# A two-layer transformer kernel on one core: first x asked for by ScalarE, edge batches' splits on VectorE, halves of the score maxima freed bank by bank, new order tables

## The reference

```python
h = _ln(x) * (1 + sc_msa) + sh_msa;  x = x + g_msa * _self_attn(h, w_qkv, ...)        # 2 windows of 128, 16 heads of 16
h = _ln(x) * (1 + sc_mca) + sh_mca;  x = x + g_mca * _topk_cross_attn(h, context, ...)
#   scores = q k / 4;  top_s, top_i = top_k(scores, 16);  softmax over these 16;  gather v
h = _ln(x) * (1 + sc_mlp) + sh_mlp;  x = x + g_mlp * _swiglu(h, ...)                   # silu(a) * b @ w_m2, hidden 1024
# layer 1: _ada_ln(x) as queries, _ada_ln(context) as keys and values, plain softmax attention, projection, residual
```

## Time and profile before

| | us |
|---|---|
| median of 3 runs | 1321.29 |
| lowest, highest | 1321.02, 1326.58 |
| the profiled execution | 1324.96 |
| its span | 1323.2 |
| PE, DVE busy | 1218.7, 1146.4 |
| ACT, POOL busy | 997.5, 882.3 |

### The profile page before, as it was taken

The page is one execution under the profiler, slowest core; times in us unless marked ns, Lnnn a source line. Parts: engine busy times, 40 slices in busy tenths (PEclk is TensorE's granted clock), DMA queues, the critical chain, the costliest instruction groups (busy, mean ns, idle before and its releaser), DMA issues. The chain is left out here.

```text
span 1323.2 us, 39161 instructions
## 1 busy us (share of the span) xinstructions
PE 1218.7 (92%) x13841; PEld 863.0 (65%) x13841; DVE 1146.4 (87%) x3819; ACT 997.5 (75%) x2001; POOL 882.3 (67%) x1161
## 2 busy tenths in 40 slices
PE   5688799999999999999999999999999999989987
PEld 5565576667676666667676767666666766656664
DVE  3359999999999999999999999999999999896222
ACT  3534587869797988979797979788797978767844
POOL 2324397858686786958595968869595957666720
PEclk9688999999999999999999999999999999999998
DMA  4450111202121121202131211212111211110010
GB/s 155 125 155 14 41 54 32 72 22 68 40 57 42 48 60 38 70 23 69 27 77 31 58 34 44 56 42 73 33 48 37 57 36 34 34 41 10 25 26 25
DMA packets 111391, 67.27 MB, mean 51 GB/s; under 512 B 13836, under 2 KB 107870, under 8 KB 111198
## 3 DMA queue, kind: packets, MB, share of 16 engines
q1 hardware_dynamic: 111198, 64.76, 18.4%
HBM read 22.33 MB, written 4.19 MB: 20 GB/s over the span
## 5 line engine op out<-in xcount | busy, mean ns | idle before, releaser
L1249 ACT ACTIVATE prob<-turned_score 128x1024 f32<-128x1024 f32 x320 | 325.9, 1018 | 107.5 <-PE turned_score L948 102.4
L1479 POOL TENSOR_TENSOR pair<-full,pair 128x512 f16<-128x512 f32 x192 | 222.2, 1165 | 129.1 <-ACT pair L1223 124.0
L1387 DVE TENSOR_REDUCE rowmax_l<-score 128x4 f32<-128x1024 f32 x128 | 156.0, 1219 | 62.6 <-PE score L948 49.4
L1400 DVE MATCH_REPLACE8 rest<-top,score 128x256 f32<-128x256 f32 x512 | 207.7, 413 | 0.0
L1414 DVE MATCH_REPLACE8 far<-best,rest 128x256 bf16<-128x256 f32 x512 | 205.2, 408 | 0.0
L1485 POOL TENSOR_SCALAR far<-far 128x512 bf16<-128x512 bf16 x256 | 158.0, 617 | 70.0 <-DVE far L1414 49.9
L1397 DVE MAX8 top<-score 128x8 f32<-128x256 f32 x512 | 192.2, 416 | 6.6 <-PE score L948 6.6
L948 PE MATMUL work<-pair_n,w_m_hi 128*128 128x256 f16 x1024 | 174.2, 275 | 1.6 <-issue 1.5
L948 PE MATMUL work<-pair_n,w_m_lo 128*128 128x256 f16 x512 | 140.3, 274 | 0.0
L1223 ACT ACTIVATE pair<-full 128x512 f16<-128x512 f32 x192 | 121.0, 630 | 17.4
L1464 POOL TENSOR_SCALAR rstd_n<-mean_var_n 128x2 f32<-128x2 f32 x64 | 13.1, 205 | 175.5 <-DVE mean_var_n L1379 173.3
(11 more groups left out here) (199 smaller groups left out, 3168.9 us busy)
## 6 DMA issues: line engine op xcount, KB each, us to landing
q_stack_w<-pair SPq DMA_DIRECT2D x96, 64.0 KB, 2.3
k_stack_w<-pair SPq DMA_DIRECT2D x96, 64.0 KB, 2.3
k_stack_t<-pair SPq DMA_DIRECT2D x96, 64.0 KB, 2.3
q_stack_t<-pair SPq DMA_DIRECT2D x96, 64.0 KB, 2.3
k_stack_l<-pair SPq DMA_DIRECT2D x96, 64.0 KB, 2.3
q_stack_l<-pair SPq DMA_DIRECT2D x96, 64.0 KB, 2.3
ctx_t<-in_ctx_turned SPq DMA_DIRECT2D x16, 256.0 KB, 2.9
ctx_l<-in_ctx SPq DMA_DIRECT2D x16, 256.0 KB, 2.9
```

The source lines that it names most:

```text
L1249: act.activation(prob[:, at:at + 2, :], both_b[:, :, :], ACT.Exp).then_inc(exp_done, 1)
L1387: dve.tensor_reduce(rowmax[s][n % 2][:, :].rearrange("p (z m) -> p z m", z=2)[:, :, at:at + wide], both_a[:, :, :].rearrange("p z (h k) -> ...
L1400: m = dve.match_replace(rest[p % 2][:, t, :], eight[:, t, :], bank[:, t * L:(t + 1) * L], -FAR)
L1479: pool.tensor_tensor(pr[:, 1, :, :], whole[:, :, :], pr[:, 0, :, :], ALU.subtract).then_inc(split_lo, 1)
```

## The change

- **First x.** Its three DMAs are no longer SP's; ACT issues them before anything else. SP's weights 0 to 6 stand ahead of the last bias and the ones, which come just before chunk 7. DVE's three instructions on the last bias move from before its loop to just before `bn_n2` of batch 0.
- **Onto VectorE** (`ON_VECTOR`): in batch 0 `lo` of n1, wk, wq, ws, n2, tq; in batch 15 `lo` of ts, n3, n4, lq, ls, and `mp`, `ml`. `mp` becomes two instructions there, (gated + 1) * linear and then * other.
- **Half the stack copies on ScalarE** (`BY_TWO`): for wk, wq, tq of batch 0 and lq of batch 15 SP issues three of six DMAs, and a new step `ia` on ACT the other three.
- **Bank by bank** (`BY_BANK`): for `w` of batch 0 and `l` of batch 15, units after the first, `a` fills one score bank after the other with a wait for each, and `rm` is two 128x512 reductions, each behind its own bank.
- **New orders.** All tables have new ticks, SHIFTS covers all sixteen batches, and WEIGHTS_AT is 0. IDLE_WORK has 32 places with 475 matmuls instead of 36 with 649. The order on PE hardly differs between batches 4 and 11; on ACT, POOL and SP neighbouring steps change places in every batch.

```diff
+ON_VECTOR = {0: ("lo_n1", "lo_wk", "lo_wq", "lo_ws", "lo_n2", "lo_tq"),
+             15: ("lo_ts", "lo_n3", "mp", "ml", "lo_n4", "lo_lq", "lo_ls")}
+BY_BANK = (("w", 0), ("l", 15))
+BY_TWO = {"wk": 0, "wq": 0, "tq": 0, "lq": 15}
+def engine_of(row, b):
+    if row[2][:3] == "ia_" and BY_TWO[row[2][3:]] != b or row[2] == "xi" and b == 0:
+        return None
+    return "dve" if row[2] in ON_VECTOR.get(b, ()) else row[1]
...
-    ("sp", "xi:0@-170.0394 in_wq:0@-33.93172 in_wk:0@-21.80413 gg_w:0@-6.59753 gg_w:1@-0.93554 gg_w:2@7.54226 "
+    ("sp", "xi:0@-167.32479 in_wq:0@-43.33762 in_wk:0@-30.36881 gg_w:0@-13.52075 gg_w:1@-11.66448 "
...
-    return {e: [(row[2], b, row[3]) for _, _, b, row in rows if row[1] == e]
+    return {e: [(row[2], b, row[3]) for _, _, b, row in rows if engine_of(row, b) == e]
...
+            for tile, dram in roll(X[0], A["x"], 0):
+                act.dma_start(tile, dram).then_inc(x_in[0], 16)
             act.wait_ge(small_in, 32)
...
                 if kind == "wd":
+                    if i == NSTAGE:
+                        for row in (0, 32):
+                            sp.dma_start(last_bias_in[row:row + 1, :], A["L1_xcond_bp"].unsqueeze(0)).then_inc(last_bias_at, 16)
+                        sp.wait_ge(ones_set, 1)
+                        for group in "wtl":
+                            for one in stack[group]:
+                                sp.dma_start(one["k"][NR:64 + NR + 1:64, :, :], ones[0:H, :]).then_inc(filled, 16)
...
+                    for rows, src in stack_parts(s, b)[:3 if BY_TWO.get(s) == b else 6]:
+                        sp.dma_start(rows, src).then_inc(in_stack[s], 16)
...
+                elif kind == "ia":
+                    act.wait_ge(split_hi, sp_no["sp_" + s, b, 0])
+                    act.wait_ge(*low_done(s, b))
...
+                    for rows, src in stack_parts(s, b)[3:]:
+                        act.dma_start(rows, src).then_inc(in_stack[s], 16)
...
+                if (piece, b) == ("bn_n2", 0):
+                    dve.wait_ge(last_bias_at, 32)
...
+                    if (s, b, i) in by_bank_no:
+                        dve.wait_ge(a_first_ready, by_bank_no[s, b, i])
+                        for z in range(2):
+                            if z == 1:
+                                dve.wait_ge(a_ready, a_no["a_" + s, b, i])
+                            dve.tensor_reduce(rowmax[s][n % 2][:, 4 * z + at:4 * z + at + wide],
+                                              bank_a[z].rearrange("p (h k) -> p h k", k=of), AX.X, ALU.max).then_inc(a_free, 1)
+                        continue
...
+                elif kind == "lo":
+                    dve.wait_ge(split_hi, sp_no["sp_" + s, b, 0])
+                    pr = pair_tile(s, b)
+                    dve.tensor_tensor(pr[:, 1, :, :], full_tile("sp_" + s, b)[:, :, :], pr[:, 0, :, :],
+                                      ALU.subtract).then_inc(edge_split_lo, 1)
+                elif kind == "mp":
...
+                    m = step(dve.scalar_tensor_tensor(gated[:, two, :], gated[:, two, :], 1.0, linear[:, two, :],
+                                                      ALU.add, ALU.mult))
+                    dve.wait_ge(dve_own, m)
+                    dve.tensor_tensor(gated[:, two, :], gated[:, two, :], other[:, two, :],
+                                      ALU.mult).then_inc(edge_gated, 1)
```

More of the change, by code:

```diff
@@ L698, in build @@
         b_no = number("pe", "b")
+        by_bank_no = {k: n + 1 for n, k in enumerate(
+            [(k[0][2:], k[1], k[2]) for k in a_no if (k[0][2:], k[1]) in BY_BANK and k[2] > 0])}
         e_no = number("act", "e")
@@ L857, in pair_freed, with stack_parts @@
             return d_ready, max(d_no[u, b, 0] for u in users)
+        def stack_parts(s, b):
+            tile = stack[s[0]][b % NS[s[0]]][s[1]]
+            return [(tile[64 * z + r * D:64 * z + (r + 1) * D, :, :], pair_tile(s, b)[:, part, z, :])
+                    for r, part in enumerate(PARTS[s[1]]) for z in range(2)]
         def roll(tile, dram, b):
@@ L879, in _ @@
             sp.dma_start(bias_col[:, :], A["bias_turned"]).then_inc(small_in, 16)
-            for row in (0, 32):
-                sp.dma_start(last_bias_in[row:row + 1, :], A["L1_xcond_bp"].unsqueeze(0)).then_inc(last_bias_at, 16)
-            sp.wait_ge(ones_set, 1)
-            for s in "wtl":
-                for one in stack[s]:
-                    sp.dma_start(one["k"][NR:64 + NR + 1:64, :, :], ones[0:H, :]).then_inc(filled, 16)
             for piece, b, i in plan["sp"]:
@@ L913, in _ @@
                         sp.wait_ge(b_ready, b_unit(st, b - NS[st], 7 if st == "w" else 15))
-                    tile = stack[st][b % NS[st]][which]
-                    for r, part in enumerate(PARTS[which]):
-                        for z in range(2):
-                            sp.dma_start(tile[64 * z + r * D:64 * z + (r + 1) * D, :, :],
-                                         pair_tile(s, b)[:, part, z, :]).then_inc(in_stack[s], 16)
+                    for rows, src in stack_parts(s, b)[:3 if BY_TWO.get(s) == b else 6]:
+                        sp.dma_start(rows, src).then_inc(in_stack[s], 16)
                 elif kind == "gg":
```

588 lines of the change are left out of this document (149 added, 439 removed), and 772 rows, old and new, of the table SHIFTS.

## The result

| | before | changed |
|---|---|---|
| median of 20 runs, us | 1321.9 | 1318.5 |
| lowest, highest | 1318.0, 1326.6 | 1312.1, 1324.3 |
| the profiled execution, its span | 1324.96, 1323.2 | 1320.78, 1318.7 |

The ratio is 0.9972, with a 95% interval from 0.9959 to 0.9986: 3.7 us faster, where 21.4 were forecast. The time lies above the range. What follows looks for the 17.7 us that are missing.

A forecast was written before the change was run, and what follows sets the result against it. VectorE and TensorE were taken as nearly full from 200 to 1100 us, with chains of waits in the first and last batch. Head −12.8, middle 0, tail −8.6: −21.4 from 1321.29 gives 1299.9 us, range 1288 to 1314.

The forecast's parts named there:

- The first x: Start of batch 0: x asked for by ACT at about 0.7, `pj_wq` at 14.9 instead of 23.43, −8.6 us.
- the last bias: Batch 0, right ahead of `bn_n2`: its three DVE instructions no longer run in idle time, +1.0 us.
- Halves of the stack copies: Window stage of batch 0: SP and ACT share the q and k stack copies, last issue earlier, −2.3 us.
- `tq` term: `bn_n2` to first top-16 scores: `pj_tq` 1.6 late, less split, SP wait and issue savings; −1.4 us, ends −3 and +3.
- Window stage: Rest of batch 0's window stage: earlier bank refills and `lo_ws` on DVE; −1.5 us, ends −3 and +1.5.
- part is given back: Rival: DVE splits meeting POOL's, an untightened exp chain and a lower clock cost 11.5 together; 1312, chance 0.13.
- The middle: 200 to 1100 us: the two full engines keep their work; 0, bounds −8 and +6.
- The four copies and splits: Last batch, last MAX8 to first scores: 1.8 and 1.9 us and two splits, 4.6 us saved.
- The last rival: Slower: POOL's new order puts mask finishing ahead of splits PE needs, 30 us over 15 batches; 1330, chance 0.06.
- The tail: Last batch, after the middle: `mp` and splits on DVE, shared stack copies, bank-wise maxima; −8.6 us.
- The term of the bank-wise maxima: Batch 15, first to last exp of eight units: bank-by-bank maxima tighten the chain, −3.5 us.

The follow-up runs named there:

- x_only: Kernel before with only the first x asked for by ScalarE, weights 0 to 6 ahead, last bias just before `bn_n2`: ratio 0.9945, 7.3 us under before.
- x_tail: x_only with the changed kernel's tail added: ratio 0.9913, 11.5 us under before, 1311.4 us.

## Why the prediction was wrong

**The first x (−8.6) and the last bias (+1.0).** Right: −9.2 at `pj_wq`, and 7.3 us of the end for the two, where the sum had 7.6. The last bias wasn't measured apart. ScalarE's three issues took 1.65, SyncE's 1.71.

**Halves of the stack copies (−2.3, and 1.9 in the `tq` term).** The first is right, 3.2 at `a_w:0`; the second brought nothing at the first top-16 scores. In time the two have 4.1, with overlapping intervals. ScalarE's three issues took 1.86, 0.62 each, which closes the gap that the sum had to bound. The Trainium skill's rule ("DMA: Bandwidth & Descriptors", section "Issuing engines are not separate DMA queues", issue time "is usually small relative to the DMA itself") would have had them near nothing; the 3.2 us at `a_w:0` decide against it for twelve small copies in a row.

**Window stage (−1.5).** Not there: `a_w:0` to `x4_n2` took 34.7 before, 36.2 in the changed kernel and 32.8 to 36.0 in the eight others with the same list, the longer the more of it TensorE spent at its lower level (7.8 to 19.2 us). The sum's upper end had the clock; the rival "part is given back" had 4 us for it, and 3.4 lie between these executions. The splits did get to 0.69, `w_co_lo` too, which took 1.64 beside GpSimd: it ran at 23.08, and GpSimd did nothing from 9.92 to 24.74. The shared port (the Trainium skill, "SBUF — State Buffer", section "Who interferes with whom") had its contender removed, and the feared loss didn't come there.

**The `tq` leg (−1.4).** The step that failed in the head. The sum let `pj_tq` inherit a wait of 1.6, on the assumption that SyncE would ask for batch 1's k stack 2.6 earlier. Counted from `x4_n2`, SyncE asked 1.6 earlier (1.3 after it, 2.9 before) and the window scores came 1.4 earlier (7.6 for 9.0), so `pj_tq` came 3.0 later than before and up to 4.0 in other traces of the list. From `x4_n2` to the first top-16 scores the sum had 15.6 (17.0 before); it took 18.9 in the changed kernel and up to 19.8. The prediction named the place and the waiting instruction, and priced it at half or less. The run without it was 4.3 faster, within overlapping intervals and with fillers gone too.

**The middle (0).** The step that failed most. Its bounds were −8 to +6; the new order cost 3.2 (0.8 to 5.6) in the kernel before, and the changed kernel is 6.9 slower with it than without, of which a part lies ahead of the joint. "The two full engines keep their work" was the error: it held for what they do and not for when. TensorE and VectorE have some 30 us of 900 to spare, and their operands come from engines whose order was new in every batch; the place at 620 shows one late operand, 3.65 us of VectorE. The last rival had the sign, with a chance of 0.06; its mechanism, GpSimd's mask finishing, isn't shown, and no other engine is shown in its place.

**The clock (in no term of its own).** The new head lost 1.0 to 5.6 us between batches 0 and 2 in nine traces (4.1 in the changed kernel's) and the two that have only its first x (x_only, x_tail) lost 0.2 at most; the sum took the whole head's gain to the end. What drives this isn't shown; it goes with the time at the lower level.

**The tail (−8.6).** −6.4 in the trace, 4.4 in time (2.0 to 6.7). The four copies and splits took 4.5 for 4.6 in this execution, 2.0 to 5.4 against before in others. The term of the bank-wise maxima was 1.1, not 3.5, and was none of the halves' doing. It was also added up wrong: 15.0 less 10.8 is 4.2, not the 4.7 that the prediction takes three quarters of.

Terms as measured: first x and last bias −7.3, halves −4.1, the order at `pj_tq` +4.3, tail −4.4, middle +6.9: −4.6, and the changed kernel has −3.7. That they nearly add up proves little: the halves and the order at `pj_tq` rest on intervals that overlap, and the +6.9 holds more than the middle. The range erred in the same place as the forecast: it took the middle's +6 for one end among many instead of adding it to the `tq` leg's +3 (−12.8 + 4.4 + 6 − 8.6 = −11.0, so 1310).

## What to carry to other kernels

Time won ahead of a stretch in which two engines are full reaches the end whole, if the order there stays as it is; x_only kept 8.7 us from 199 to 848. The clock at the start of the stretch belongs to that "as it is": every trace of the new head lost part of its lead there. A new order in such a stretch is a change of its own, with a price of its own, and has to be tried alone before it is sent along with mechanisms. And where a step is put behind another that waits, it starts only when the other's operand lands; read that time, and then what still stands behind it: 4 us at `pj_tq` were 1 to 2 at the scores after it.
